# First swap of q and k on TensorE, factors' maximum over all partitions, split reload, and a second tile without a copy, in an attention and mixture-of-experts kernel

## The reference

```python
def reference(x, ctx_2048, g_xattn, g_ffn, ...):            # x, ctx: (8, 256, 512)
    x = x + tanh(g_xattn[0]) * xattn(layernorm(x), ctx, ctx, encoding, Wq, bq, ...)
    x = x + tanh(g_ffn[0]) * moe(layernorm(x), gate_w, w0, w1, wo)

def xattn(query, key, value, encoding, ...):
    q, k, v = (einsum('oi,bin->bon', W, t) + b for each).reshape(b, 16, 16, n)
    q, k = (t * encoding[0] + rotate_half(t) * encoding[1] for t in (q, k))
    prob = softmax(einsum('bdhn,bdhm->bhnm', q, k) / 4)
    return Wm @ einsum('bhnm,bdhm->bdhn', prob, v).reshape(b, 256, n) + bm

def moe(x, gate_w, w0, w1, wo):                             # 2048 tokens, 8 experts, top 2
    cw = softmax of the two largest of x @ gate_w, 0 elsewhere
    return sum(cw[:, e:e + 1] * ((silu(x @ w0[e]) * (x @ w1[e])) @ wo[e]) for e in range(8))
```

## Time and profile before

| | us |
|---|---|
| median of 3 runs | 1141.71 (1136.63 to 1145.53) |
| the profiled execution | 1141.93 |
| its span, first to last instruction | 1139.8 |
| TensorE busy | 1084.0 |
| VectorE busy | 801.2 |
| ScalarE busy | 685.3 |
| GpSimd busy | 378.3 |

### The profile page before, as it was taken

One profiled execution on the slowest core, in us unless ns is written; L12 is line 12 of the kernel. 1 busy time (PEld: TensorE's weight loads), 2 busy tenths in 40 slices (PEclk: granted clock), 3 DMA queues, 4 the chain that ended last, 5 costly groups with the idle time before them and its releaser, 6 DMA issues.

```text
span 1139.8 us, 18978 instructions
## 1 busy us (share of the span) xinstructions
PE 1084.0 (95%) x5965; PEld 441.7 (39%) x5965; DVE 801.2 (70%) x1597; ACT 685.3 (60%) x934; POOL 378.3 (33%) x489
## 2 busy tenths in 40 slices
PE   7898999999999999998989999999999999999997
PEld 3322333333333333332344444444444444444443
DVE  6967898898988897879367575657557565655632
ACT  2266777777777777778766474646446464653421
POOL 3671745858484764522220111111111101111101
PEclk9988999999999999989989999999999999999999
DMA  6325634323234323201268685758658576773443
GB/s 209 119 71 176 216 107 169 116 88 117 79 113 133 112 79 103 76 26 67 89 225 268 147 193 104 212 129 218 149 82 216 123 219 142 203 168 58 73 58 46
DMA packets 182702, 150.98 MB, mean 132 GB/s; under 512 B 122704, under 2 KB 143952, under 8 KB 182608
## 3 DMA queue, kind: packets, MB, share of 16 engines
q1 hardware_dynamic: 172240, 129.63, 39.7%
q0 software_dynamic: 7456, 17.57, 8.1%
q10 hardware_dynamic: 2912, 2.61, 0.7%
HBM read 73.67 MB, written 41.23 MB: 101 GB/s over the span
## 4 chain that ended last, share of the span: by engine, by line
PE 76%; DVE 11%; ACT 7%; issue 4%; DMA 2%; SPq 0%; POOL 0%; DVEq 0%; POOLq 0%; ACTq 0%
PE psum L1272 37%; PE psum L1273 10%; PE psum L351 7%; PE psum L338 6%; ACT W L525 5%; PE psum L235 5%; DVE MX L716 5%; PE psum L326 3%; PE psum L278 3%; PE psum L245 2%; PE psum L1266 1%; PE psum L260 1%; ACT W L475 1%; PE psum L296 1%; PE psum L266 1%
## 5 line engine op out<-in xcount | busy, mean ns | idle before, releaser
L525 ACT ACTIVATE W<-psum,es 128x512 f32<-128x512 f32 x512 | 321.5, 688 | 75.6 <-PE psum L338 74.0
L716 DVE TENSOR_REDUCE MX<-psum 128x2 f32<-128x1024 f32 x256 | 310.5, 1219 | 58.3 <-PE psum L326 56.0
L1272 PE MATMUL psum<-W,xT 128*128 128x512 f16 x1296 | 284.2, 379 | 2.0 <-DVE xT L1424 2.0
L1272 PEld LDWEIGHTS psum<-W,xT 128*128 128x128 f16 x1296 | 125.9, 98 | 156.7 <-issue 5.4
L338 PE MATMUL psum<-stg 50*128 50x512 f16 x512 | 145.2, 394 | 20.5 <-ACT W L525 16.2
L1533 POOL DMA_INDIRECT out<-yb,target x34 | 53.1, 1562 | 292.7 <-ACT yb L1366 290.2
L1465 DVE TENSOR_TENSOR hh<-sg,psum 128x512 f32<-128x512 f32 x68 | 46.4, 686 | 144.7 <-ACT sg L1353 144.7
L1272 PE MATMUL psum<-W,hT 128*128 128x512 f16 x648 | 144.4, 379 | 0.2 <-ACT hT L1331 0.2
L351 PE MATMUL psum<-W 128*32 128x512 f32 x1024 | 141.2, 624 | 0.0
L1353 ACT ACTIVATE sg<-psum,i 128x512 f32<-128x512 f32 x68 | 46.3, 681 | 142.7 <-PE psum L1272 120.1
L599 DVE SCALAR_TENSOR_TENSOR W<-stg,scw,W 128x1024 f16<-128x1024 f32 x96 | 117.3, 1280 | 12.0 <-ACT W L592 12.0
(11 more groups left out here) (237 smaller groups left out, 1338.1 us busy)
## 6 DMA issues: line engine op xcount, KB each, us to landing
stg<-in_w SPq DMA_DIRECT2D x16, 2048.0 KB, 9.3
stg<-in_wo SPq DMA_DIRECT2D x8, 2048.0 KB, 10.4
stg<-scr SPq DMA_DIRECT2D x186, 64.0 KB, 2.3
Xs<-zero SPq DMA_DIRECT2D x40, 264.0 KB, 3.1
W<-W SPq DMA_DIRECT2D x64, 128.0 KB, 2.1
scr<-W SPq DMA_DIRECT2D x32, 256.0 KB, 3.1
xs<-in_x SPq DMA_DIRECT2D x8, 512.0 KB, 4.2
out<-xs SPq DMA_DIRECT2D x8, 512.0 KB, 3.0
```

The lines of the kernel that those rows point to most:

```text
L525: act.activation(m.Pb[:, c % 2, hh, :], m.psT[tile % 2], ACT.Exp, scale=m.es[:, hb // 2:hb // 2 + 1]).then_inc(S["exped"], 1)
L716: dve.tensor_reduce(m.MX[:, hb % 2, c0:c0 + 9:8], m.psS[tile % 2], AX_X, ALU.max, negate=True).then_inc(S["maxed"], 1)
L1272: return pe.matmul(out, rows, m.wh[(e % 2, w)][:, wp, cols], start=start, stop=stop)
```

## The change

1. The first exchange of neighbouring rows, of q and of k of half batch 0, is done by TensorE: `swap_first` multiplies `qb` by a permutation matrix `swap`, loaded from DRAM, into PSUM banks 5 and 3, and the rotation reads it there. SP's four DMAs for it go.
2. The maximum of the rotation factors is taken from `fx`, the same factors spread over all partitions, 128 of them in each, loaded in addition to `fT`. `rope_in` now counts five loads.
3. The six reload DMAs of the first k are issued three by SP, three by ScalarE.
4. Filler: 36 instead of 26 ahead of phase -1, 3 more at step 9 of it, and 2 at each of the first three steps of phase 0.
5. Experts: tile 1 of expert 0 is read where it is loaded, in `xg`, and tile 2 is loaded into `xT`; VectorE's two copies become empty instructions. TensorE waits for `hidden` by halves. At the very end the transposes no longer wait for ScalarE's copy of bank 6.

```diff
+SWAPPED = (5, 3)
...
+        self.fx, self.swap = sb("fx", [128, 2, 64]), sb("swap", [128, 128])
...
+    def swap_first(w):
+
+        evacuated(pe, S, ("qk"[w], 0))
+        pe.wait_ge(S["rope_in"], 80)
+        pe.matmul(m.psum[:, SWAPPED[w], :], m.swap[:, :], m.qb[:, w, :], start=True, stop=True).then_inc(S[f"swapped{w}"], 32)
...
-            early(26)
+            early(36)
...
-                if ph == -1 and s in (2, 5, 8, 12, 13, 14, 15):
+                if ph == -1 and s in (2, 5, 8, 9, 12, 13, 14, 15):
                     early(3)
+                if ph == 0 and s < 3:
+                    early(2, m.psV)
+                if ph == -2 and s == 0:
+                    swap_first(0)
+                    swap_first(1)
...
-def stack(eng, m, S, w, hb):
+def stack(eng, m, S, w, hb, us=(0, 1)):
...
-        for u in range(2):
+        for u in us:
...
-    step(eng.tensor_tensor(m.qs[:, w, :], m.qs[:, w, :], m.fT[:, 1, :], ALU.mult))
+    step(eng.tensor_tensor(m.qs[:, w, :], m.qs[:, w, :] if hb else m.psum[:, SWAPPED[w], :], m.fT[:, 1, :], ALU.mult))
...
-    for dst, nm in ((m.bq, "bq"), (m.fT, "fT"), (m.sgn, "sgn")):
+    for dst, nm in ((m.bq, "bq"), (m.fx, "fx"), (m.fT, "fT"), (m.swap, "swap"), (m.sgn, "sgn")):
         load(dst, nm, "rope_in")
...
     stack(act, m, S, 0, 0)
+    stack(act, m, S, 1, 0, (1,))
     job("k", 1)
...
-        step.more(dve.tensor_reduce(m.big[:, 4:6], m.fT[:, :, :], AX_X, ALU.max, apply_absolute_value=True))
+        step.more(dve.tensor_reduce(m.big[:, 4:6], m.fx[:, :, :], AX_X, ALU.max, apply_absolute_value=True))
...
-    swap(0, 0)
-    swap(1, 0)
     keep(0, 0)
     swap(0, 1)
     keep(1, 0)
-    stack(sp, m, S, 1, 0)
+    stack(sp, m, S, 1, 0, (0,))
...
+            second = e == 0 and mark == "second"
+            rows = m.xg if second else m.xT
             if P is None:
                 pe.wait_ge(S["first_rows"], 16)
+            elif second:
+                pe.wait_ge(S["rows_in"], 32)
             else:
                 pe.wait_ge(S["x_in"], T + 1)
-            passed(pe, S, "hidden", T * 2)
-            if parity is not None:
-                pe.nop().then_inc(S["pe_step"], 1)
             for j in range(2):
+                if P is not None:
+                    pe.wait_ge(S["hidden"], T * 2 - 1 + j)
+                if parity is not None:
+                    pe.nop().then_inc(S["pe_step"], 1)
...
-            passed(pe, S, "result_out", P)
+            if mark != "end":
+                passed(pe, S, "result_out", P)
             for hp in range(2 if mark == "end" else 0):
...
+            if mark == "end":
+                pe.wait_ge(S["result_out"], P)
...
-        dve.tensor_copy(m.xT[:, :, :], m.xg[:, :, :]).then_inc(S["x_in"], 1)
+        if e == 0 and mark in ("first", "second"):
+            dve.nop().then_inc(S["x_in"], 1)
+        else:
+            dve.tensor_copy(m.xT[:, :, :], m.xg[:, :, :]).then_inc(S["x_in"], 1)
...
-            passed(sp, S, "x_in", T + 1)
+            second = e == 0 and mark == "second"
+            if second:
+                sp.wait_ge(S["gated"], 2)
+            else:
+                passed(sp, S, "x_in", T + 1)
...
-                    load_rows(rows, m.xg, part, "rows_in")
+                    load_rows(rows, m.xT if second else m.xg, part, "rows_in")
...
+    a["fx"] = x["L0_xattn_encoding"].reshape(2, 128, 64).transpose(1, 0, 2)
+    a["swap"] = np.eye(128, dtype=np.float32)[np.arange(128) ^ 1]
```

More of the change, by code:

```diff
@@ L360, in busy, with early @@
             pe.matmul(m.psum[:, 1, :], m.ones[:, :], m.wh[(0, 0)][:, 0, 512 * (i % 8):512 * (i % 8) + 512], start=True, stop=True)
-    def early(n):
+    def early(n, bank=m.psT[0]):
         pe.wait_ge(S["dve_step"], 1)
+        if bank is m.psV:
+            evacuated(pe, S, ("k", 0))
         for i in range(n):
-            pe.matmul(m.psT[0], m.zero[:, 0:64].bitcast(F16), m.zero[:, 0:256].bitcast(F16), start=True, stop=True)
+            pe.matmul(bank, m.zero[:, 0:64].bitcast(F16), m.zero[:, 0:256].bitcast(F16), start=True, stop=True)
     EARLY_IDLE = {("q", 0): 20, ("k", 1): 24}
@@ L465, in projected @@
         act.wait_ge(S["projected"], 2 * hb + w + 1)
-        act.wait_ge(S["rope_in"], 48)
+        act.wait_ge(S["rope_in"], 80)
         if hb:
@@ L900, in largest @@
     def largest():
-        dve.wait_ge(S["rope_in"], 48)
+        dve.wait_ge(S["rope_in"], 80)
         step.more(dve.tensor_reduce(m.big[:, 2:4], m.bq[:, :, :], AX_X, ALU.max, apply_absolute_value=True))
-        step.more(dve.tensor_reduce(m.big[:, 4:6], m.fT[:, :, :], AX_X, ALU.max, apply_absolute_value=True))
+        step.more(dve.tensor_reduce(m.big[:, 4:6], m.fx[:, :, :], AX_X, ALU.max, apply_absolute_value=True))
         step.settle()
@@ L1131, in sync_attention @@
     load_ctx(sp, m, S, io, 0)
-    sp.wait_ge(S["rope_in"], 48)
+    sp.wait_ge(S["rope_in"], 80)
     load_x(sp, m, S, io, 1)
@@ L1294, in step @@
                         c = k * 1024 + j * 512
-                        last = both(parity, e, m.psum[:, 2 * j + w, :], m.xT[:, 4 * xp + k, :], w, wp, slice(c, c + 512),
+                        last = both(parity, e, m.psum[:, 2 * j + w, :], rows[:, 4 * xp + k, :], w, wp, slice(c, c + 512),
                                     start=(k == 0 and xp == 0 and wp == 0), stop=(k == 3 and xp == 1))
@@ L1419, in hold, with rows_in @@
         dve.tensor_copy(m.held[:, :], m.number[:, :]).then_inc(S["held"], 1)
-    def rows_in(T, e):
+    def rows_in(T, e, mark):
         passed(dve, S, "rows_in", T * 32 + 32 * e)
-        dve.tensor_copy(m.xT[:, :, :], m.xg[:, :, :]).then_inc(S["x_in"], 1)
+        if e == 0 and mark in ("first", "second"):
+            dve.nop().then_inc(S["x_in"], 1)
+        else:
+            dve.tensor_copy(m.xT[:, :, :], m.xg[:, :, :]).then_inc(S["x_in"], 1)
     def blend(out, mine, other, e):
@@ L1466, in step @@
         if nxt is not None:
-            rows_in(T + 1, e + 1 if mark == "last" else e)
+            rows_in(T + 1, e + 1 if mark == "last" else e, mark)
         hm = m.hm
```

## The result

The changed kernel took 1138.43 us (median of 22 runs, 1135.81 to 1143.84), the kernel before on the same chip 1144.28 (22 runs, 1136.63 to 1149.11): a ratio of 0.9956, with a 95% interval of 0.9942 to 0.9969, or 5 us. The prediction had 1137.8 us, a gain of 4.1 us, and 0.89 on "within 1%". The time and the sum came out right, in part by luck: the kernel before, at 1141.71 us in the three runs that the sum started from, has 1144.28 in 22. Of the reasons behind the sum, those for the start and for tile 1 did not hold, and the clock was priced from a stretch longer than most; they are most of what follows.

A forecast was written before the change was run, and what follows sets the result against it. TensorE, busy 95% of the span, was taken as the bound. Start +0.3, fillers +0.6, clock -3.9, tile 1 -0.8, nops +0.5 and end -0.8 sum to -4.1 from 1141.93, giving 1137.8 us; range 1131.0 to 1144.0.

The forecast's parts named there:

- The data line of the start: Start, maxima to reloaded rows: maximum 0.28 us, q's rotation at 17.2, all stacked rows at about 30.2, 3.3 us gained.
- Both stay ahead of 34 us: Start: k's next copy on ScalarE waits behind three more issues, but it and SP's next swap stay ahead of 34 us.
- All spent waiting behind filler: Start, TensorE: the data line's 3.3 us gain is all spent behind filler, which ends at 34.1 us.
- Term +0.3 for the start: First score at about 34.0 us instead of 33.67, held by TensorE's projections and filler; bounds -0.2 and +1.
- The clock, -3.9, and fillers, +0.6: Phases -1 and 0: the low clock stretch at 60.2 goes, -3.9 us; added fillers cost +0.6 (0.4 to 1.3).
- Rival A: Near 60 us: filler does not hold the clock, the -3.9 goes, 1141.7 us; chance 0.28.
- rival B: Early phases: both low clock stretches go, -2.6 us more, 1135.2 us; chance 0.12.
- Rival C: Ahead of the first score: filler runs at half rate, 5.1 us lost, 1146.8 us; chance 0.05.
- D: Start: reload lands later than 34 us because the longer set of loads holds back what waits for it; chance 0.05.
- Tile 1, -0.8: Expert 0: the 2.04 us hole ahead of tile 1 loses 0.6 to 0.9, then released by the notes load.
- Second nop, +0.5: First tile of experts 1 to 7: split wait for hidden brings a second nop, +0.5 us (0 to 0.7).
- The end, -0.8: Last transposes: upper half fills TensorE's 0.90 us wait; last product starts at about 1127.85 instead of 1128.62.

The follow-up runs named there:

- e8: Whole change with run-time checks, but all six reload DMAs of the first k on SP, against the kernel before: ratio 0.9957, mean 1139.3 us.
- e12: Start parts alone with run-time checks, ScalarE's three reload DMAs moved behind its k1 copy and root, against the kernel before: ratio 0.9982, mean 1141.8 us.
- e5: Whole change with run-time checks, but 26 instead of 36 fillers ahead of phase -1, against the kernel before: ratio 0.9969, mean 1141.6 us.
- e3: Filler alone (part 4) with run-time checks, added to the kernel before and compared with it: ratio 0.9991, mean 1143.0 us.
- e4: Experts alone (part 5) with run-time checks, added to the kernel before and compared with it: ratio 0.9973, mean 1141.8 us.
- e1: Whole change with run-time checks of the registers its waits use, against the kernel before: ratio 0.9965, mean 1140.1 us.
- e7: Whole change with run-time checks, without filler at step 9 of phase -1 and in phase 0, against the kernel before: ratio 0.9995, mean 1143.5 us.
- e2: Start alone (parts 1 to 3) with run-time checks, added to the kernel before and compared with it: ratio 1.0005, mean 1144.8 us.
- e10: Whole change with checks, reload all on SP, tile 1's notes early, 26 fillers ahead of phase -1, against the kernel before: ratio 0.9924, mean 1134.9 us.
- e11: As e10, but three reload DMAs on ScalarE behind its k1 copy and root, against the kernel before: ratio 0.9945, mean 1137.5 us.
- e6: Whole change with run-time checks, tile 1's notes load issued directly behind its rows, against the kernel before: ratio 0.9948, mean 1138.0 us.
- e9: Whole change with run-time checks, all six reload DMAs on SP and tile 1's notes early, against the kernel before: ratio 0.9966, mean 1140.3 us.

## Why the prediction came out right, step by step

- **The data line of the start.** The maximum, 0.28 us, and the rotation, 17.48 (17.2 said), were right; product with PSUM 0.69 as taken. The last stacked row was there at 32.0, not at 30.2: k's write began at 24.19 (23.9 said) and the last of the nine issues of ScalarE ended at 28.56, but the rows took 3.4 us more to land, where I had taken the 2.39 us of the earlier trace rows for a last reload. The filler covered it. (The 32.0 is when ScalarE, which waits for all rows, issues its next load, `stg<-in_ctx`.)
- **"Both stay ahead of 34 us".** This step failed. I followed ScalarE's copy of k1 to SP's swap, and not to what is queued behind it on ScalarE: the root, for which VectorE waits, and behind that the norm, for which TensorE and the first maximum wait. Three issues of 0.45 us, and the 1.2 us for which ScalarE waits ahead of them, moved the root by 0.72 us; the norm behind it took 0.90 longer, and VectorE's first maximum went from 34.10 to 35.27. e8 and e12, with those issues elsewhere, have it at 34.90 behind an idle 2.96 us, and at 32.80. The number for the first score (34.0, measured 34.72) hid this, since filler ended at the same time.
- **"All spent waiting behind filler".** Half right. Filler held the score (no idle before it), but e5 shows that taking it away alone brings phase 0 forward by 0.5 us and the time not at all.
- **Term +0.3 for the start:** +1.05 at the first score, at the edge of its bounds. 0.4 of it is the first x, landing at 7.03 instead of 6.64; the profiles of e3 and e4, whose start loads are as before, have 7.01 and 7.04, so it is scatter and not the two added loads. Another 0.3 is the clock: q's first projection ran at the lower level in this execution (3.62 us, before 1.98), so that k's came at 14.41 (12.42), and ScalarE's copy of it waited 0.56 us. The delay does not stay at 1.05: phase 0 begins 1.7 us later than before and its first weighting 2.05 later (e1: 1.0 and 1.4), where the sum had 0.9 for start and filler together.
- **The clock, -3.9, and fillers, +0.6:** net -3.3 predicted, with the whole 3.9 us between 11.39 and 7.47 taken off, as if filler kept the granted clock at 1.00 through that piece in every execution; e3 alone gave -1.8 ± 0.7, taking the late filler away cost 3.5 ± 1.1 (e7). The stretch at 60 is gone from all profiles with late filler. The price of the piece was right to 0.2 us (11.39 to 7.27). The -3.9 was this stretch at its longest: the same piece took 11.39 us with 10.2 us at the lower level (before), 9.74 with 6.8 (e7, e12), 8.36 and 8.35 with 3.4 (e2, e4) and 7.27 with none, so it cost 1.1, 2.5 or 4.1 us. How often before has which, one profile cannot say; that the term was mis-sized is the likelier reading of e3's -1.8. There are stretches elsewhere, in this profile eight short ones, and they come and go: this page's one low digit is a stretch of 10.2 us at 581.2, in before at 582.6. Rival A, that filler holds nothing, falls; rival B, both stretches gone, did not come: the one near 103 us was 3.4 us long instead of 6.8 here, but 6.8 in e3, e5, e10 and e11, which have the filler too. Rival C, filler at half rate ahead of the score, happened in no profile; D neither.
- **Tile 1, -0.8:** measured 2.04 - 1.31 = -0.73, and the releaser as named, but this is the luck of one profile. I took the notes' issue time from before as if it moved with TensorE. It hangs on SP's own line, behind the padding rows, and in e1, e4, e5, e7 and e8 the hole was 2.08 to 3.03, of which the checks explain 0.3: at best 0.3 us of gain, and in e5 and e8 a loss. The notes moved forward (e6, e9, e10, e11) close it.
- **Second nop, +0.5:** nothing. The second wait costs nothing either: from 609 to 1120 us TensorE's product groups have 0.0 us of idle time ahead of them, and the sequencer gets to a wait early (L1311 at 620.4, 46 ns, while products run from 618.63 on and the gates start at 623.81). On the chain the first mixed tile takes 655.05 to 665.53 = 10.48 us, and before 657.07 to 667.55 = 10.48.
- **The end, -0.8:** from transposes' start to the last product's it was 1.59 us (1124.26 to 1125.85) and the 0.90 us ahead are gone; VectorE's half costs 0.38 in the middle. With the 0.90 us and the 1.28 that stood there before, that is -0.6; in e1 and e6 VectorE's half costs 0.74, which leaves -0.4. From the totals to the end of the span the change takes 550.9 us, before 552.7: -1.8 for tile 1, nops and end, where the terms add to -1.1.

The sum of the two halves: totals at 585.95 against 587.10 is -1.15 (predicted -3.0), the rest -1.8 (predicted -1.1). So in the profiled pair, 2.9 us apart in their spans, the attention stage gave less than said and the experts more. e1's profile of the same program has it the other way round, -2.8 and -0.5. Over the runs it is 5 us. No single pair of profiles could have decided this: within one kernel the runs spread by 8 us.

## What to carry to other kernels

Where an issue of a DMA is moved to an engine that computes, follow that engine's own queue to the end: the reader that waits may not be that of the instruction right behind it. Look also for what the issue itself waits for: the engine stands still for that too, 1.2 us here. Two limits that end within a microsecond of each other can each look worthless when taken away alone; before a part of a change is called useless, take its twin away too. Here filler kept TensorE's clock up as nine products of 0.217 us, three in the phase ahead of the fall and six in the phase of it (e7), and ten more in front of the loop did nothing for it (e5: mean clock 0.985, with them 0.984 in e1). And before a cost is read from one profile of a stretch at the lower clock, look how long that stretch is in other executions.

## What the runs showed of the hardware

TensorE's granted clock is a property of a kernel only as a mean: in the 29 runs of the kernel before on the third chip it was 0.974 to 0.987. Within the runs of each kernel (235 in all) a microsecond more at the lower level goes with 0.28 us more time, with a correlation of 0.69 (a correlation, not the measured cost of a stretch: in phase 0 it was 0.3 to 0.4 us for each, from the durations above); one execution has 31 to 48 us of it on the average of its kernel. The stretches lie near the same places in the fourteen profiles, among them 98 to 105, 166 to 172, 489 to 496 and 578 to 585 us; what differs is which of them a profile has, and whether one is 3.4, 6.8 or 10.2 us long. The stretches differ between executions of the same instructions too: e8 and e9 run one program up to the end of attention, and near 168 e8 has 6.8 us at the lower level and e9 none, near 492 e8 has 3.4 and e9 10.2.

VectorE's norm of the second x, two instructions, took 2.77 us here and 1.13 us in e7. GpSimd tells them apart: in the change it works beside it nearly without a gap, in e7 it pauses from 32.33 to 33.66. e1 is the other profile with 1.13 us, and with such a pause (33.24 to 34.01); in the remaining twelve, with GpSimd at work beside it, the norm took 1.69 to 2.95 us.

```profile
31.19 1.16 POOL L465 TENSOR_TENSOR W<-W 128x512 f16<-128x512 f32 x1
32.60 1.27 POOL L461 TENSOR_TENSOR W<-W 128x512 f32<-128x512 f32 x1 [0.25 <-POOL W L465]
33.94 1.32 POOL L462 TENSOR_TENSOR W<-W 128x512 f32<-128x512 f32 x1
```

```profile
32.69 1.13 DVE L695 TENSOR_SCALAR W<-xs,mv,rstd 128x512 f32<-128x512 f32 x2
```

```profile
31.18 1.15 POOL L463 TENSOR_TENSOR W<-W 128x512 f16<-128x512 f32 x1
33.66 1.27 POOL L459 TENSOR_TENSOR W<-W 128x512 f32<-128x512 f32 x1 [1.33 <-issue]
```

So the norm took 0.56 us or more longer where GpSimd worked beside it. That GpSimd's work is the cause is my reading of these durations: no row shows how the one would slow the other, and no run here moved GpSimd's work to test it.
